# Weights subtracted a quarter earlier, candidate tiles laid out cell by cell, two one-column copies gone, in a one-core audio tower kernel

## The chip, the cores and the metric

One core of a Trainium2 chip runs the whole program. The metric is device time in microseconds. The engines are PE (TensorE), ACT (ScalarE), DVE (VectorE), POOL (GpSimd) and SP (SyncE, which issues the DMAs). Each works through its own list of instructions in order and meets the others at semaphores.

## The reference

The input is 32 clips of 40000 samples. The output has a row of 128 for each of 313 frames of each clip.

```python
h = _L0_tok_ref(x)                                  # frames of 128 samples, each times a DCT basis
h = h + _L0_attn_ref(_layernorm(h, axis=-1))        # softmax(x x^T) x inside each clip
h = h + _L0_ffn_ref(_layernorm(h, axis=-1), ...)    # below; H = 8 heads, K = 16, 64 keys a half
...
s0 = einsum(_l2norm(q0), _l2norm(keys0)); s1 = einsum(_l2norm(q1), _l2norm(keys1))
sc0, ix0 = top_k(s0, K); sc1, ix1 = top_k(s1, K)
cs = (sc0[..., :, None] + sc1[..., None, :]).reshape(b, s, H, K * K)
ci = (ix0[..., :, None] + ix1[..., None, :]).reshape(b, s, H, K * K)
fs, pos = top_k(cs, K)
fi = take_along_axis(ci, pos, axis=-1)
w = softmax(fs, axis=-1)
out = einsum('bshk,bshko->bso', gelu(<hidden, expert_down[fi]>) * w, expert_up[fi])
```

The index of an expert is the sum of two numbers below 64, so only experts 0 to 126 are used.

## The kernel before

The clips are worked in 16 pairs. A pair is 626 rows, cut into NT = 5 tiles of 128 rows (t = 0 to 4; the last overlaps). All engines follow one written order, `drive`: for each pair k, tile t and quarter p = 0 to 3 they do `slot(k, t, p)`, the feed-forward part, and then `front(k + 1, t, p)`, the DCT, attention and projection of the next pair. What an engine does in a quarter is given by `if p == ...` lines in its own `slot`, so the order of the lines sets the order of its work.

A tile goes through the slots with a lag. `exists(k, t, lag)` says that slot t works on the tile of `lag` slots ago:

- Lag -1: PE makes `SC`, the scores of all 16 half heads against their keys, and ACT copies them into `sraw`.
- Lag 0, DVE, p = 1 and 2: the best 16 of 64 for each half head (`vals`, `idx`), by MAX8, MATCH_REPLACE8 into `hrest`, MAX8, and two FIND_INDEX8.
- Lag 1: POOL builds 54 candidate sums a head, `cs` (p = 0) and `ci` (p = 1), with `cells`, five instructions each. DVE (p = 3) takes the best 16 of the 54: a MAX8 into `top`, MATCH_REPLACE8 into `crest`, MAX8, and MATCH_REPLACE8 into `c2`, eight of each, one a head. In `c2` each picked candidate has the value PICKED. The profile calls `c2` just `c`.
- Lag 2: ACT makes `zexp`, the mask `m` out of `c2`, and `wexp` = exp(cs) (p = 0). POOL (p = 2) makes `wz` = wexp times 1/sum, `Yw` = wz times m, and `Ye` = ci times m in bf16. PE (p = 3, in `rows`) turns Ye into the bank `EB` and Yw into the bank `U`, both with cells on partitions.
- Lag 3: ACT makes `hi` out of EB (p = 0), DVE makes `lo`, `alpha` and `beta` out of it (p = 1). The weights in U are split into three bf16 parts: ACT copies `wp` part 0 out of U, PE subtracts it in U by a matmul with `minusb` (`less(buf, 0)`), ACT copies part 1, PE subtracts it, ACT copies part 2. This is the subtraction chain, with semaphores w1_full, rest1_full, w2_full, rest2_full, w3_full. POOL (p = 3) multiplies the three parts with beta into `bw`, three instructions, waiting for w3_full.
- Lag 4: PE multiplies alpha and bw into `QB`, 16 matmuls a quarter ("quads"), and ACT copies each quarter into `WD`.
- Lag 5: POOL sums WD and multiplies it with the gelu values into `G`, ACT spreads G into `Gd`, PE multiplies with the expert rows and adds the residual (`FO`, in a QB bank), ACT copies to `ofin`, SP stores it.

In the front part `FB` is a pair of PSUM banks that PE and ACT hand to and fro: transposes, the attention's S (L421) and O (L429), in slot t = 3 at p = 0 the projection L440 with ACT's squares `sq` (L656), at (3, 2) the matmuls for variances and norms (L449 and L450, here called VAR), which DVE waits for at `v` (L985).

All candidate tiles except Yw and Ye have the layout [128, H, NC], 54 candidates of a head side by side. Yw and Ye are [128, NC, H], and the multiplications write them with a step.

Of the kernel before, what the change touches and what calls it, by code (L numbers as in the profile page):

```python
# [11 lines left out]
ALU = mybir.AluOpType  # L12
# [9 lines left out]
NT = 5  # L22
# [6 lines left out]
NC = 54  # L29
# [50 lines left out]
def build(nc, x, Wq, bq, ln_g, ln_b, keys0, keys1, down, up, ident_d, dct_d, indc_d, sel_d, row8_d, sel3_d, out):  # L80
# [4 lines left out]
    with ctx:  # L85
# [77 lines left out]


        sraw = sb("sraw", [128, 3, 1024])
        mark = sb("mark", [128, 2 * NT])
        hrest = sb("hrest", [128, 1024])
        vals = sb("vals", [128, 3, 16, TOP])
        idx = sb("idx", [128, 3, 16, TOP], U32)
        idxf = sb("idxf", [128, 16, TOP])  # L170
        vs = sb("vs", [128, 16, TOP])
        cs = sb("cs", [128, 3, H, NC])
        ci = sb("ci", [128, 3, H, NC])
        crest = sb("crest", [128, H, NC])
        c2 = sb("c2", [128, H, NC])
        top = sb("top", [128, H, TOP])
        zexp = sb("zexp", [128, H, TOP])
        zs = sb("zs", [128, H])
        rz = sb("rz", [128, H])
        m = sb("m", [128, H, NC])  # L180
        wexp = sb("wexp", [128, H, NC])
        wz = sb("wz", [128, H, NC])
        Yw = sb("Yw", [128, NC, H])
        Ye = sb("Ye", [128, NC, H], BF16)
        wp = sb("wp", [128, 3, 3, 256], BF16)
# [186 lines left out]
        def _(pe):  # L372
# [130 lines left out]
            def slot(k, t, p):  # L503
                n = NT * k + t
                if p == 0 and t == NT - 1 and exists(k, 0, 0):
                    inner(k)
                if p == 1 and exists(k, t, -1):
                    k1, t1 = (k, t + 1) if t < NT - 1 else (k + 1, 0)
                    scores(k1, t1)
                if p == 1 and exists(k, t, 3):  # L510
                    pe.wait_ge(s["w1_full"], n - 2)
                    less(RING[(t - 3) % NT], 0).then_inc(s["rest1_full"], 1)
                if p == 2 and exists(k, t, 3):
                    pe.wait_ge(s["w2_full"], n - 2)
                    less(RING[(t - 3) % NT], 1).then_inc(s["rest2_full"], 1)
                if p == 3 and exists(k, t, 5):

                    after(pe, s["wd_full"], 4 * (n - 4) + 2 if exists(k, t, 4) else 4 * NTILES)
                    pe.wait_ge(s["gd_full"], n - 4)
                    pe.wait_ge(res_full[RING[t]], 16 * ring_use(k - 1, t) + 16)  # L520
                    for y in range(NY):
                        mm(FO, Gd[:, y, :], upR[:, y, :], start=(y == 0), stop=False)  # L522
                    mm(FO, ident[:], res[:, RING[t], :], start=False, stop=True).then_inc(s["fo_full"], 1)
                if exists(k, t, 4):
                    buf = RING[(t - 4) % NT]
                    if p == 0:
                        pe.wait_ge(s["alpha_full"], n - 3)
                        pe.wait_ge(s["bw_full"], n - 3)
                    bank = QB[p % 2]
                    after(pe, s["wd_full"], 4 * (n - 4) + p - 1)  # L530
                    bwv = bw[:, buf, :, :].rearrange("p s (a g q) -> p s a g q", a=2, g=NG)
                    for u in range(8):
                        for a in range(2):
                            last = mm(bank[:, 48 * u:48 * u + 48], alpha[:, buf, a, :, 8 * p + u],  # L534
                                      bwv[:, :, a, :, 8 * p + u], start=(a == 0), stop=(a == 1))
                    last.then_inc(s["quads_full"], 1)
                if p == 3 and exists(k, t, 2):
                    after(pe, s["lo_full"], n - 2)
                    pe.wait_ge(s["y_full"], n - 1)
                    rows(Ye, identb, STE, True).then_inc(s["eb_full"], 1)  # L540
                    after(pe, s["w3_full"], n - 2)
                    rows(Yw, ident, U[:, 0:256], False).then_inc(s["st_full"], 1)
# [33 lines left out]
        def _(act):  # L576
# [91 lines left out]
            def slot(k, t, p):  # L668
# [7 lines left out]
                if p == 0 and exists(k, t, 2):  # L676
                    buf = RING[(t - 2) % NT]
                    act.wait_ge(s["c2_full"], n - 1)
                    after(act, s["zs_full"], n - 2)
                    A(zexp[:], top[:], ACT.Exp).then_inc(s["zexp_full"], 1)  # L680
                    after(act, s["y_full"], n - 2)
                    A(m[:], c2[:], ACT.Relu, scale=-1.0, bias=cpick[:]).then_inc(s["m_full"], 1)
                    after(act, s["wz_full"], n - 2)
                    A(wexp[:], cs[:, buf, :, :], ACT.Exp).then_inc(s["wexp_full"], 1)
                if p == 0 and exists(k, t, 3):
                    buf = RING[(t - 3) % NT]
                    act.wait_ge(s["st_full"], n - 2)
# [22 lines left out]
                if p == 1 and exists(k, t, -1):  # L710
# [1 line left out]
                    act.wait_ge(s["scores_full"], n + 2)  # L712
                    after(act, s["halves_full"], n)
                    A(sraw[:, buf, :], SC[:], ACT.Copy).then_inc(s["sraw_full"], 1)  # L714
                if p == 1 and exists(k, t, 3):
                    act.wait_ge(s["rest1_full"], n - 2)
                    A(wp[:, RING[(t - 3) % NT], 1, :], U[:, 0:256], ACT.Copy).then_inc(s["w2_full"], 1)  # L717
                if p == 2 and exists(k, t, 3):
                    act.wait_ge(s["rest2_full"], n - 2)
                    A(wp[:, RING[(t - 3) % NT], 2, :], U[:, 0:256], ACT.Copy).then_inc(s["w3_full"], 1)  # L720
                if exists(k, t, 4):
                    act.wait_ge(s["quads_full"], 4 * (n - 4) + p + 1)
                if p == 3 and exists(k, t, 5):
# [4 lines left out]
                if exists(k, t, 4):  # L728
                    if p == 0:
                        after(act, s["ws_steps"], 2 * (n - 5))  # L730
                    blocks = QB[p % 2][:, 0:384].rearrange("p (u s g) -> p s u g", u=8, g=NG)
                    for g in range(NG):
                        r = slice(32 * g, 32 * g + 32)
                        last = A(WD[r, RING[(t - 4) % NT], :, 8 * p:8 * p + 8], blocks[r, :, :, g], ACT.Copy)  # L734
                    last.then_inc(s["wd_full"], 1)

            def late(t, p):
                if (t, p) == (0, 0):
# [15 lines left out]
        def _(pool):  # L754
# [79 lines left out]
            def cells(dst, v, done):  # L834

                halves = v.rearrange("p (h a) r -> p h a r", a=2)
                for i0, ni, nj, off in CAND:
                    by = "p h (j i) -> p h i j" if i0 == 4 else "p h (i j) -> p h i j"
                    o = dst[:, :, off:off + ni * nj].rearrange(by, i=ni)
                    a0 = halves[:, :, 0, i0:i0 + ni].unsqueeze(3).to_broadcast([128, H, ni, nj])  # L840
                    a1 = halves[:, :, 1, 0:nj].unsqueeze(2).to_broadcast([128, H, ni, nj])
                    last = tt(o, a0, a1, ALU.add)  # L842
                last.then_inc(done, 1)


            def slot(k, t, p):
# [10 lines left out]
                if p == 0 and exists(k, t, 1):  # L857
                    buf = RING[(t - 1) % NT]
                    pool.wait_ge(s["halves_full"], n)
                    kk, t1 = (k, t - 1) if t else (k - 1, NT - 1)  # L860
                    pool.wait_ge(s["rn_steps"], 12 * kk + 12)
                    after(pool, s["cs_full"], n - 1)
                    tt(vs[:], vals[:, buf, :, :], rn[:, 16 * t1:16 * t1 + 16].unsqueeze(2).to_broadcast([128, 16, TOP]), ALU.mult
                       ).then_inc(s["vs_full"], 1)
                    pool.wait_ge(s["vs_full"], n)
                    after(pool, s["wexp_full"], n - 2)
                    cells(cs[:, buf, :, :], vs[:], s["cs_full"])
                if p == 0 and t == 0 and exists(k, t, 0):
                    pool.wait_ge(s["seed4_full"], k + 1)
                    newton(y4[:], xh4[:], na[:], c15[:], s["rn_steps"], 12 * k, rn[:])  # L870
# [6 lines left out]
                if p == 2 and exists(k, t, 2):  # L877
                    buf = RING[(t - 2) % NT]
                    pool.wait_ge(s["rz_full"], n - 1)
                    pool.wait_ge(s["wexp_full"], n - 1)  # L880
                    tt(wz[:], wexp[:], rz[:].unsqueeze(2).to_broadcast([128, H, NC]), ALU.mult).then_inc(s["wz_full"], 1)
                    pool.wait_ge(s["wz_full"], n - 1)
                    pool.wait_ge(s["m_full"], n - 1)
                    after(pool, s["st_full"], n - 2)
                    for Y, src in ((Yw, wz[:]), (Ye, ci[:, buf, :, :])):
                        last = tt(Y[:].rearrange("p c h -> p h c"), src, m[:], ALU.mult)  # L886
                    last.then_inc(s["y_full"], 1)
                if p == 3 and exists(k, t, 3):
                    buf = RING[(t - 3) % NT]
# [13 lines left out]
        def _(dve):  # L903
# [103 lines left out]
            def slot(k, t, p):  # L1007
                n = NT * k + t
                if p == 0 and exists(k, t, 0):


                    dve.wait_ge(s["sraw_full"], n + 1)
                    after(dve, s["cs_full"], n - 1)
                    after(dve, s["idxf_full"], n - 1)
                    V.tensor_copy(mark[:, t:t + 1], ident[:, 0:1])
                if exists(k, t, 0) and p in (1, 2):
                    buf = RING[t]
                    chain = s["top_chain"]
# [48 lines left out]
                if p == 3:  # L1067
                    if exists(k, t, 1):
                        buf = RING[(t - 1) % NT]
                        dve.wait_ge(s["cs_full"], n)  # L1070
                        after(dve, s["wexp_full"], n - 1)
                        V.tensor_copy(mark[:, NT + t:NT + t + 1], ident[:, 0:1])
                        chain = s["cand_chain"]
                        for h in range(H):
                            V.max(top[:, h, 0:8], cs[:, buf, h, 0:NC8]).then_inc(chain, 1)
# [5 lines left out]
                            V.max(top[:, h, 8:16], crest[:, h, :]).then_inc(chain, 1)  # L1081
                        for h in range(H):
                            dve.wait_ge(chain, 2 * H + h + 1)
                            V.match_replace(c2[:, h, :], top[:, h, 8:16], crest[:, h, :], PICKED
                                            ).then_inc(chain if h < H - 1 else s["c2_full"], 1)
                    if exists(k, t, 0):
                        dve.wait_ge(s["top_chain"], 79)
# [89 lines left out]
```

## Time and profile before

| what | value |
|---|---|
| median of 3 runs | 2089.96 us (2086.35 to 2092.89) |
| the profiled execution | 2086.75 us |
| its span, first to last instruction | 2084.9 us |
| mean granted clock of TensorE | 0.77 of full |
| DVE busy | 1924.9 us, 92% |
| PE busy | 1702.7 us, 82% |
| POOL busy | 1561.5 us, 75% |
| ACT busy | 1214.0 us, 58% |

Busy times are shares of the whole span. The span has a beginning of about 110 us and an end of about 75 us in which not every engine has work. Instructions of one engine overlap at their ends, so an instruction's own duration is longer than what it takes of its engine's queue; the distance to the start of the next tells that.

### The profile page before, as it was taken

How to read it: one execution, taken by the hardware profiler on the slowest of the kernel's cores; microseconds unless marked ns; L12 is line 12 of the kernel's file. 1: busy time of each engine (PE TensorE's matmuls, PEld its weight loads, DVE VectorE, ACT ScalarE, POOL GpSimd, SP SyncE). 2: the span in 40 equal slices, each digit the busy share in tenths (PEclk: the TensorE clock that was granted, in tenths of full speed). 3: DMA queues.
4: the chain of work that ended last, by engine and by line, in shares of the span. 5: the costliest groups of instructions: out<-in, count | busy, mean ns of one | idle time of the engine just before them, and what ended most of it. 6: DMA issues, size and time to landing. Idle time of an engine off the chain costs nothing.

```text
span 2084.9 us, 49107 instructions
## 1 busy us (share of the span) xinstructions
PE 1702.7 (82%) x11935; PEld 1301.7 (62%) x11935; DVE 1924.9 (92%) x15878; ACT 1214.0 (58%) x3835; POOL 1561.5 (75%) x2561
## 2 busy tenths in 40 slices
PE   5567888878888888888888888888888888798766
PEld 3335576756767676675667667576665767567556
DVE  3299999999999999999999999999999999999992
ACT  3345656666565656656566665666665566665454
POOL 2238787886868788686878868778777878878765
PEclk9676878778777877887788678778867887787666
DMA  1000000000000000000000000000000000000000
GB/s 35 13 9 2 19 7 8 19 7 19 7 19 7 7 19 9 19 7 18 7 6 19 9 17 8 13 13 6 19 7 18 9 13 13 6 13 9 7 6 11
DMA packets 46676, 24.93 MB, mean 12 GB/s; under 512 B 4955, under 2 KB 46116, under 8 KB 46390
## 3 DMA queue, kind: packets, MB, share of 16 engines
q1 hardware_dynamic: 46390, 21.80, 3.8%
q8 instruction: 96, 1.57, 0.3%
q14 instruction: 190, 1.56, 0.2%
HBM read 11.52 MB, written 10.26 MB: 10 GB/s over the span
## 4 chain that ended last, share of the span: by engine, by line
PE 43%; DVE 23%; ACT 18%; POOL 10%; issue 5%; SPq 0%; another core or an unknown queue 0%; DMA 0%; POOLq 0%; DVEq 0%; ACTq 0%
PE QB L534 9%; PE FB L449 5%; PE SC L483 5%; ACT WD L734 4%; PE FB L440 4%; PE QB L522 4%; DVE alpha L1048 4%; DVE idx L1032 3%; DVE idx L1035 3%; DVE hrest L1026 3%; PE FB L429 3%; ACT hi L674 3%; PE FB L421 2%; POOL sa L764 2%; PE FB L397 2%
## 5 line engine op out<-in xcount | busy, mean ns | idle before, releaser
L894 POOL TENSOR_TENSOR bw<-beta,wp 128x1024 bf16<-128x1024 bf16 x240 | 508.0, 2147 | 121.3 <-ACT wp L720 121.3
L534 PE MATMUL QB<-bw,alpha 128*128 128x48 bf16 x5120 | 554.1, 277 | 32.2 <-issue 32.2
L534 PEld LDWEIGHTS QB<-bw,alpha 128*128 128x128 bf16 x5120 | 522.1, 151 | 69.9 <-issue 60.9
L734 ACT ACTIVATE WD<-QB 32x96 f32<-32x96 f32 x1280 | 307.0, 240 | 77.6 <-PE QB L534 66.1
L1048 DVE TENSOR_SCALAR alpha<-hi 128x1024 bf16<-128x1024 bf16 x640 | 276.0, 503 | 0.0
L483 PE MATMUL SC<-WK,hidT 128*128 128x512 f32 x320 | 228.8, 805 | 50.2 <-ACT stdT L666 36.3
L1032 DVE FIND_INDEX8 idx<-vals,sraw 128x8 uint32<-128x64 f32 x1280 | 250.9, 219 | 0.0
L1035 DVE FIND_INDEX8 idx<-vals,hrest 128x8 uint32<-128x64 f32 x1280 | 250.5, 219 | 0.0
L1026 DVE MATCH_REPLACE8 hrest<-vals,sraw 128x64 f32<-128x64 f32 x1280 | 249.6, 207 | 0.0
L842 POOL TENSOR_TENSOR ci<-idxf 128x64 f32<-128x64 f32 (+3 forms) x400 | 124.0, 345 | 121.2 <-DVE beta L1054 121.1
L727 ACT ACTIVATE ofin<-QB 128x128 f32<-128x128 f32 x80 | 22.2, 277 | 282.3 <-PE QB L534 279.6
L842 POOL TENSOR_TENSOR cs<-vs 128x64 f32<-128x64 f32 (+3 forms) x400 | 172.5, 467 | 6.3
L886 POOL TENSOR_TENSOR Ye<-ci,m 128x432 bf16<-128x432 f32 x80 | 174.8, 2186 | 0.0
L1023 DVE MAX8 vals<-sraw 128x8 f32<-128x64 f32 x1280 | 169.1, 208 | 0.0
L1030 DVE MAX8 vals<-hrest 128x8 f32<-128x64 f32 x1280 | 167.2, 207 | 0.0
L483 PEld LDWEIGHTS SC<-WK,hidT 128*128 128x128 f32 x320 | 72.9, 247 | 110.9 <-issue 54.4
L714 ACT ACTIVATE sraw<-SC 128x1024 f32<-128x1024 f32 x80 | 83.0, 1037 | 99.8 <-PE SC L484 99.0
L440 PE MATMUL FB<-hidTn,WcT 128*128 128x313 f32 x256 | 112.1, 589 | 34.2 <-ACT sq L656 23.4
L522 PE MATMUL QB<-upR,Gd 128*128 128x128 f32 x640 | 134.6, 378 | 4.5 <-issue 4.2
L674 ACT ACTIVATE hi<-EB,cdig 128x256 bf16<-128x256 f32 x320 | 124.9, 475 | 22.8 <-PE EB L494 21.7
L501 PE MATMUL U<-wp,minusb 128*128 128x256 bf16 x160 | 51.0, 319 | 103.1 <-ACT wp L717 71.7
L522 PEld LDWEIGHTS QB<-upR,Gd 128*128 128x128 f32 x640 | 123.6, 284 | 9.1 <-issue 7.7
(206 smaller groups left out, 3999.2 us busy)
## 6 DMA issues: line engine op xcount, KB each, us to landing
res<-h_scratch SPq DMA_DIRECT2D x80, 64.0 KB, 1.8
xin<-in_x SPq DMA_DIRECT2D x32, 128.0 KB
h_scratch<-h2n SPq DMA_DIRECT2D x32, 128.0 KB
out<-ofin SPq DMA_DIRECT2D x64, 64.0 KB, 1.5
h_scratch<-h2n SPq DMA_DIRECT2D x32, 28.5 KB
out<-ofin SPq DMA_DIRECT2D x16, 57.0 KB
xin<-in_x SPq DMA_DIRECT2D x32, 28.0 KB
xin<-in_x SPq DMA_DIRECT2D x32, 0.2 KB
```

Of the source, the lines that this page charges most:

```text
L440: mm(bank[:, 0:NF], WcT[:, 128 * c:128 * c + 128], hidTn[:, NF * b:NF * b + NF], start=True, stop=True).then_inc(f_full[c % 2], 1)
L483: mm(SC[:, cols], hidT[:, START[t1]:START[t1] + 128], WK[:, cols], start=True, stop=False)
L522: mm(FO, Gd[:, y, :], upR[:, y, :], start=(y == 0), stop=False)
L534: last = mm(bank[:, 48 * u:48 * u + 48], alpha[:, buf, a, :, 8 * p + u], bwv[:, :, a, :, 8 * p + u], start=(a == 0), stop=(a == 1))
L674: last = A(hi[:, c, :], STE, ACT.Identity, bias=cdig[:, c:c + 1])
L734: last = A(WD[r, RING[(t - 4) % NT], :, 8 * p:8 * p + 8], blocks[r, :, :, g], ACT.Copy)
L842: last = tt(o, a0, a1, ALU.add)
L894: last = tt(bw[:, buf, NY * i:NY * i + NY, :], beta[:, buf, :, :], wp[:, buf, i, :].unsqueeze(1).to_broadcast([128, NY, 256]), ALU.mult)
L1026: V.match_replace(rest[i], vals[:, buf, i, 0:8], raw[i], -1e30).then_inc(chain, 1)
L1032: V.max_index(idx[:, buf, i, 0:8], vals[:, buf, i, 0:8], raw[i]).then_inc(chain, 1)
L1035: last = V.max_index(idx[:, buf, i, 8:16], vals[:, buf, i, 8:16], rest[i])
L1048: last = V.tensor_scalar(a8[:, :, :, xx, :], h8, BASE + float(NY * xx), None, ALU.is_equal)
```

## The change

Three things are changed. First, `c2`, `ci`, `m`, `wexp` and `wz` get the layout [128, NC, H], a cell's eight heads side by side, as Yw and Ye have it already. `m`, `wz`, Yw and Ye become plain products of 432 values in a row. The instructions that write `c2` (DVE), `wexp` (ACT) and `ci` (POOL) now step by 8 values, 32 bytes, between neighbours; `cs` stays as it was. Second, the subtraction chain is one quarter earlier: `less(buf, 0)` and the copy of part 1 go from the start of p = 1 to the end of p = 0, `less(buf, 1)` and the copy of part 2 from the start of p = 2 to the end of p = 1. Third, DVE's copies into `mark`, one column each, two a slot, are gone, and `mark` with them.

```diff
-        mark = sb("mark", [128, 2 * NT])
...
-        ci = sb("ci", [128, 3, H, NC])
+        ci = sb("ci", [128, 3, NC, H])
         crest = sb("crest", [128, H, NC])
-        c2 = sb("c2", [128, H, NC])
+        c2 = sb("c2", [128, NC, H])
...
-        m = sb("m", [128, H, NC])
-        wexp = sb("wexp", [128, H, NC])
-        wz = sb("wz", [128, H, NC])
+        m = sb("m", [128, NC, H])
+        wexp = sb("wexp", [128, NC, H])
+        wz = sb("wz", [128, NC, H])
...
# PE, slot
-                if p == 1 and exists(k, t, 3):
-                    pe.wait_ge(s["w1_full"], n - 2)
-                    less(RING[(t - 3) % NT], 0).then_inc(s["rest1_full"], 1)
-                if p == 2 and exists(k, t, 3):
-                    pe.wait_ge(s["w2_full"], n - 2)
-                    less(RING[(t - 3) % NT], 1).then_inc(s["rest2_full"], 1)
...
                     last.then_inc(s["quads_full"], 1)
+                if p == 0 and exists(k, t, 3):
+                    pe.wait_ge(s["w1_full"], n - 2)
+                    less(RING[(t - 3) % NT], 0).then_inc(s["rest1_full"], 1)
+                if p == 1 and exists(k, t, 3):
+                    pe.wait_ge(s["w2_full"], n - 2)
+                    less(RING[(t - 3) % NT], 1).then_inc(s["rest2_full"], 1)
...
# ACT, slot
-                    A(wexp[:], cs[:, buf, :, :], ACT.Exp).then_inc(s["wexp_full"], 1)
+                    A(wexp[:].rearrange("p c h -> p h c"), cs[:, buf, :, :], ACT.Exp).then_inc(s["wexp_full"], 1)
...
# ACT: the copies of wp parts 1 and 2 move as on PE, to behind the WD copies of p = 0 and p = 1
...
# POOL, cells
-                    by = "p h (j i) -> p h i j" if i0 == 4 else "p h (i j) -> p h i j"
-                    o = dst[:, :, off:off + ni * nj].rearrange(by, i=ni)
+                    by = "p (j i) h -> p h i j" if i0 == 4 else "p (i j) h -> p h i j"
+                    o = dst[:, off:off + ni * nj, :].rearrange(by, i=ni)
...
# POOL, slot
-                    tt(wz[:], wexp[:], rz[:].unsqueeze(2).to_broadcast([128, H, NC]), ALU.mult).then_inc(s["wz_full"], 1)
+                    tt(wz[:], wexp[:], rz[:].unsqueeze(1).to_broadcast([128, NC, H]), ALU.mult).then_inc(s["wz_full"], 1)
...
-                        last = tt(Y[:].rearrange("p c h -> p h c"), src, m[:], ALU.mult)
+                        last = tt(Y[:], src, m[:], ALU.mult)
...
# DVE, slot
-                    V.tensor_copy(mark[:, t:t + 1], ident[:, 0:1])
...
-                        V.tensor_copy(mark[:, NT + t:NT + t + 1], ident[:, 0:1])
...
-                            V.match_replace(c2[:, h, :], top[:, h, 8:16], crest[:, h, :], PICKED
+                            V.match_replace(c2[:, :, h], top[:, h, 8:16], crest[:, h, :], PICKED
```

On ACT, slot t = 3 from `wexp` on: before, then with the change. Line numbers are those of each kernel's own text; the names after a wait are its semaphores.

```order
L684 ACTIVATE wexp<-cs 128x432 [waits wz_full]
L689 ACTIVATE wp<-U 128x256 [waits bw_full,st_full]
L701 ACTIVATE idxf<-idx,cquart 128x256 [waits ci_full,halves_full]
L734 ACTIVATE WD<-QB 32x12x8 [waits ws_steps,quads_full]
L734 ACTIVATE WD<-QB 32x12x8 x3
L656 ACTIVATE sq<-FB,bqc 128x313 [waits f0_full]
...
L714 ACTIVATE sraw<-SC 128x1024 [waits halves_full,scores_full]
L717 ACTIVATE wp<-U 128x256 [waits rest1_full]
L734 ACTIVATE WD<-QB 32x12x8 [waits quads_full]
L734 ACTIVATE WD<-QB 32x12x8 x3
L720 ACTIVATE wp<-U 128x256 [waits rest2_full]
```

With the change:

```order
L683 ACTIVATE wexp<-cs 128x8x54 [waits wz_full]
L688 ACTIVATE wp<-U 128x256 [waits bw_full,st_full]
L700 ACTIVATE idxf<-idx,cquart 128x256 [waits ci_full,halves_full]
L727 ACTIVATE WD<-QB 32x12x8 [waits ws_steps,quads_full]
L727 ACTIVATE WD<-QB 32x12x8 x3
L731 ACTIVATE wp<-U 128x256 [waits rest1_full]
L655 ACTIVATE sq<-FB,bqc 128x313 [waits f0_full]
...
L713 ACTIVATE sraw<-SC 128x1024 [waits halves_full,scores_full]
L727 ACTIVATE WD<-QB 32x12x8 [waits quads_full]
L727 ACTIVATE WD<-QB 32x12x8 x3
L734 ACTIVATE wp<-U 128x256 [waits rest2_full]
```

The copy of part 1 has moved ahead of the front's `sq` and of `sraw`; the copy of part 2 stands right behind the WD copies of p = 1, ahead of whatever front work there is. `wexp` has a three-dimensional output.

On PE, a slot t = 0 from the first quads on, before:

```order
L534 MATMUL QB<-bw,alpha 128x48 [waits wd_full,bw_full,alpha_full]
L534 MATMUL QB<-bw,alpha 128x48 x15
L483 MATMUL SC<-WK,hidT 128x512 [waits sraw_full,gelu_full,stdT_full,hidT_full]
L484 MATMUL SC<-bKs,stdT 128x512
L483 MATMUL SC<-WK,hidT 128x512
L484 MATMUL SC<-bKs,stdT 128x512
L501 MATMUL U<-wp,minusb 128x256 [waits w1_full]
L534 MATMUL QB<-bw,alpha 128x48 [waits wd_full]
L534 MATMUL QB<-bw,alpha 128x48 x15
L501 MATMUL U<-wp,minusb 128x256 [waits w2_full]
```

The same place with the change:

```order
L527 MATMUL QB<-bw,alpha 128x48 [waits wd_full,bw_full,alpha_full]
L527 MATMUL QB<-bw,alpha 128x48 x15
L500 MATMUL U<-wp,minusb 128x256 [waits w1_full]
L482 MATMUL SC<-WK,hidT 128x512 [waits sraw_full,gelu_full,stdT_full,hidT_full]
L483 MATMUL SC<-bKs,stdT 128x512
L482 MATMUL SC<-WK,hidT 128x512
L483 MATMUL SC<-bKs,stdT 128x512
L527 MATMUL QB<-bw,alpha 128x48 [waits wd_full]
L527 MATMUL QB<-bw,alpha 128x48 x15
L500 MATMUL U<-wp,minusb 128x256 [waits w2_full]
```

The first subtraction, with its wait for w1_full, now stands ahead of the scores. The second is at the end of its quarter instead of the start of the next; in slot t = 1 the 18 attention matmuls L429 lie between these two places.

## Rows read from the trace of the kernel before

**Rows 1.** The page: busy shares by engine; the chain's shares by engine.
```profile
PE 1702.7 (82%) x11935; PEld 1301.7 (62%) x11935; DVE 1924.9 (92%) x15878; ACT 1214.0 (58%) x3835; POOL 1561.5 (75%) x2561
...
PE 43%; DVE 23%; ACT 18%; POOL 10%; issue 5%; SPq 0%; another core or an unknown queue 0%; DMA 0%; POOLq 0%; DVEq 0%; ACTq 0%
```

**Rows 2.** Busy us of PE, PEld, DVE, ACT, POOL in one window; clock, DMA.
```profile
110.00:2010.00 1900.00, 1587.34 (x11283) 1216.76 (x11282) 1851.53 (x15427) 1139.49 (x3594) 1481.29 (x2396) 0.78 0.04 11
```

**Rows 3.** Waits: who waited for whom, us in total, times, longest.
```profile
PE EB L490 <- POOL Ye L886: 42.9, 19, 4.6
...
DVE v L985 <- PE FB L450: 38.3, 15, 21.6
...
DVE lo L1042 <- ACT hi L674: 35.8, 27, 9.1
```

**Rows 4.** The chain in order of time, one slot t=3: start, us, what.
```profile
1007.28 0.45 ACT wexp L684
1007.73 0.28 ACT wp L689
...
1009.29 0.53 ACT sq L656
```

**Rows 5.** The chain: first and last piece of wexp, Ye, c, U.
```profile
269.95 0.45 ACT wexp L684
...
2024.21 0.45 ACT wexp L684
...
332.26 2.11 POOL Ye L886
...
1807.15 2.08 POOL Ye L886
...
122.91 0.47 DVE c L1084 x3
...
2021.83 1.50 DVE c L1084 x9
...
276.01 0.12 PE U L501
...
2058.82 0.40 PE U L501
```

**Rows 6.** Timeline of DVE at a slot's end, and two groups of MAX8.
```profile
1001.41 0.19 DVE L1084 MATCH_REPLACE8 c<-top,crest 128x54 f32<-128x54 f32 x1
1001.53 0.14 DVE L1015 COPY mark<-ident 128x1 f32<-128x1 f32 x1
1001.59 0.21 DVE L1023 MAX8 vals<-sraw 128x8 f32<-128x64 f32 x1
...
L1081 DVE MAX8 top<-crest 128x8 f32<-128x54 f32 x640 | 81.5, 201 | 0.0
...
L1075 DVE MAX8 top<-cs 128x8 f32<-128x38 f32 x640 | 70.8, 184 | 0.0
```

**Rows 7.** Groups of POOL's products: busy us, mean ns, idle before, releaser.
```profile
L894 POOL TENSOR_TENSOR bw<-beta,wp 128x1024 bf16<-128x1024 bf16 x240 | 508.0, 2147 | 121.3 <-ACT wp L720 121.3
...
L886 POOL TENSOR_TENSOR Ye<-ci,m 128x432 bf16<-128x432 f32 x80 | 174.8, 2186 | 0.0
...
L886 POOL TENSOR_TENSOR Yw<-wz,m 128x432 f32<-128x432 f32 x80 | 90.2, 1127 | 6.3
...
L881 POOL TENSOR_TENSOR wz<-wexp,rz 128x432 f32<-128x432 f32 x80 | 72.7, 909 | 2.3 <-DVE rz L1066 2.3
...
L851 POOL TENSOR_TENSOR ws<-WD 128x128 f32<-128x128 f32 x80 | 39.6, 495 | 23.3 <-ACT WD L734 23.3
```

**Rows 8.** Timelines: DVE's alpha twice, and bw in a slot t=1.
```profile
1007.05 3.51 DVE L1048 TENSOR_SCALAR alpha<-hi 128x1024 bf16<-128x1024 bf16 x8
...
1106.22 2.76 DVE L1048 TENSOR_SCALAR alpha<-hi 128x1024 bf16<-128x1024 bf16 x8
...
1096.40 6.32 POOL L894 TENSOR_TENSOR bw<-beta,wp 128x1024 bf16<-128x1024 bf16 x3 [5.20 <-ACT wp L720]
```

More of the change, by code:

```diff
@@ L714, in slot @@
                     A(sraw[:, buf, :], SC[:], ACT.Copy).then_inc(s["sraw_full"], 1)
[L715 to L720, printed above, removed]
                 if exists(k, t, 4):
@@ L735, in slot @@
                     last.then_inc(s["wd_full"], 1)
+                if p == 0 and exists(k, t, 3):
+                    act.wait_ge(s["rest1_full"], n - 2)
+                    A(wp[:, RING[(t - 3) % NT], 1, :], U[:, 0:256], ACT.Copy).then_inc(s["w2_full"], 1)
+                if p == 1 and exists(k, t, 3):
+                    act.wait_ge(s["rest2_full"], n - 2)
+                    A(wp[:, RING[(t - 3) % NT], 2, :], U[:, 0:256], ACT.Copy).then_inc(s["w3_full"], 1)
             def late(t, p):
@@ L866, in slot @@
                     after(pool, s["wexp_full"], n - 2)
-                    cells(cs[:, buf, :, :], vs[:], s["cs_full"])
+                    cells(cs[:, buf, :, :].rearrange("p h c -> p c h"), vs[:], s["cs_full"])
                 if p == 0 and t == 0 and exists(k, t, 0):
```

## The prediction

> **What bounds the kernel now.** I read the page's engine shares first, then one long window, then the waits, then the chain of work that ended last. VectorE (DVE) is busy 1924.9 of 2084.9 us, PE 1702.7, and the chain still runs mostly through PE, 43%, with DVE 23%, ACT 18% and POOL 10% of it [rows 1]. The window from 110 to 2010 us shows why one should not stop at the 92%: there DVE is busy 1851.5 of 1900 us, 97.4%, and idles 48.5 us in all [rows 2]. The other idle time lies in the first 110 and the last 75 us. So two lines of work are nearly tied. One is DVE's own queue. The other goes PE, ACT, PE, ACT inside each slot and meets DVE where DVE waits: for `hi` before `lo` (35.8 us, 27 times) and for the VAR matmuls before `v` (38.3 us, 15 times) [rows 3]. In the chain's own order the second line shows its links: after `hi` come `m`, `wexp` (0.45), the first `wp` copy (0.28), then WD, and only then `sq` at 1009.29, whose FB bank the next projection matmul takes [rows 4]. A longer `wexp`, or one more ACT instruction ahead of `sq`, moves all of that.
>
> How often each touched instruction is a link, counted over the chain of the whole span: `wexp` in 39 pieces, one a slot, from 269.95 to 2024.21; Ye in 12, from 332.26 to 1807.15; the c2 replacements in 28 pieces of 23.8 us together, which at 1.47 us for one slot's eight is 16 slots or 130 replacements; the subtraction matmuls on U in 69 pieces of 9.8 us [rows 5]. A change of a link's length, times its count, is the first estimate of the change of the span. The DVE queue is a second account, which may grow only until its 48.5 us of idle are used, if the waits let it.
>
> **The two copies.** One stands between a replacement that starts at 1001.41 and the MAX8 behind it: the copy starts at 1001.53, MAX8 at 1001.59, so it takes 0.06 us of DVE's queue, though its row says 0.14 [rows 6]. I take as much for both kinds: 160 x 0.06 = 9.6 us off DVE's account, and, with DVE 23% of the chain, 2 us off the chain. The waits they carried go to the first MAX8, so no wait changes.
>
> **Steps of 32 bytes.** c2 is now written one head at a time into [NC, H]: 54 values, each 32 bytes behind the last. So is `wexp`, 432 values, by ACT, and `ci` by POOL. No row of DVE or ACT shows such a write. Contiguous, a DVE replacement of 54 takes 0.12 us from its start to the next load [rows 6]. The nearest rows are POOL's. Yw is written in just these steps and takes 1127 ns for 432 values, 2.6 ns each; `wz`, contiguous with one full-length input, takes 909; `ws` with two full inputs takes 495 for 128, so Yw may be slow from reading alone [rows 7]. Ye is the row that speaks for a price: two-byte values at 16-byte steps take 2186 ns, 5.1 ns each, where contiguous `bw` takes 2147 for 1024, 2.1 ns each [rows 7]. A writer that hops can therefore be the limit here. The bounds: below, nothing; above, one write every 2.6 ns, all of Yw. A gain has no reason, since nothing else of these instructions changes. ACT: `wexp` (432 values) and `wp` (256) differ by 0.17 us, 0.97 ns a value [rows 4], so the bound is (2.6 - 0.97) x 432 = +0.70 us. DVE: MAX8 over 54 and over 38 values differ by 17 ns, 1.06 ns a value [rows 6], so the bound is 1.54 x 54 = +83 ns a replacement. I take 0.64 for ACT, whose instruction is long (a little under the bound, since some of Yw's 1127 ns is its start), and 60 ns for DVE, where some writes can finish under the next value load, because Ye's row is nearer to a price than to none. Chain: 39 x 0.64 = +25.0; 130 x 0.060 = +7.8. DVE's account: 640 x 0.060 = +38.4.
>
> The Trainium skill, Vector Engine (DVE) Microarchitecture Reference, section Measured stream behaviour, speaks against this edit outright: a DVE port keeps its full rate only in runs of two or more adjacent words, and a destination that steps 24 words every element took 2.50 ns a column where contiguous took 1.05. By that page the replacements would cost 1.45 x 54 = 78 ns each, an estimate, +50 us on DVE's account instead of 38. No run here shows it yet.
>
> **Y, wz and ci on POOL.** Ye loses its steps and becomes a product of the shape of Yw: 2186 - 1127 = 1.06 us shorter, with a lower end of 2186 - 909 = 1.28 [rows 7]. Yw keeps two full inputs; 0 to -0.2, taken as 0. `wz` stays. `ci` gets steps: 0 to +0.2 us a tile (the 909 to 1127 gap), taken 0.1. PE waited 42.9 us for Ye in 19 slots [rows 3], and it is a link in 12: 12 x (1.06 - 0.1) = -11.5 us. The other 68 tiles' gain is POOL idle, for POOL is busy 78% of the window [rows 2].
>
> **The subtraction chain.** Each of its four instructions goes one step of the order earlier. Where the change pays is POOL: `bw` waited 121.3 us for the third `wp` copy [rows 7], nearly all in slots t=1, where the O matmuls stood between: `bw` starts at 1096.40 after 5.20 us idle [rows 8]. Now it can start right behind Ye. But that wait is not on the chain, where `bw` hardly occurs; what it brings is that POOL's cs work is over before `alpha` starts in t=2. There eight `alpha` take 3.51 us beside cs, and 2.76 us where they are alone [rows 8]: 0.75 x 16 = -12 us at best on DVE's account, 9 taken. On PE the first subtraction leaves the place between the scores and the second group of quads: half of its 9.8 us of links, -5. It now waits ahead of the front's matmuls for the first `wp`, until 1008.0 in [rows 4], so PE stands there longer; what hides it is that `sq` at 1009.29 has yet to free the FB bank. If that cover went, PE would lose about the length of `wexp` and `wp`, 0.7 us a slot, or 1.3 with the price above. On ACT the second `wp` copy now stands ahead of `sq`, E or hidT: +0.28 [rows 4] in the slots where these are links, three of four of the 39, +8.1. In t=2 ACT is the link all through and order changes nothing.
>
> **The sum.** Chain: +25.0 + 7.8 - 2 - 11.5 - 5 + 8.1 = +22.4 us. DVE's account: +38.4 - 9.6 - 9 = +20, which fits under 48.5. The profiled execution took 2086.75 us with a span of 2084.9, so about 2109 by that execution; the median of the three runs is 3.2 us above it. Forecast 2112 us, 1.1% slower.
>
> **The rivals.**
> - *Steps are free* (faster). Place: the port writes of c2, `wexp`, `ci`. For it: POOL's `ws` explains Yw without them. Then 22.4 - 25.0 - 7.8 - 1.2 = -11.6: 2078 us, and 2070 if DVE's 18 us come through in full. It decides from the price per value: the rest of the sum is -11.6, the stepped links are 39 x 432 + 130 x 54 = 23,900 values, so below 0.48 ns extra per value the kernel gets no slower. Chance 0.25.
> - *Half the price* on both engines: 0.32 x 39 + 0.03 x 130 + 0.6 - 11.6 = +5: 2095 us. Chance 0.15.
> - *Only DVE pays.* The long ACT instruction hides its writes. Chain -2.6, DVE's account +20, partly under its idle: 2087 to 2095, 2090. Chance 0.08.
> - *The lines add.* DVE's 20 us and the chain's 22 do not overlap, because the chain changes lines several times in five slots; or the subtraction, waiting for `wp`, holds up the scores in t=0. +42: 2132 us. For it: the tie is close, 48.5 us in 80 tiles. Chance 0.10.
> - The forecast: 0.42, own range 2102 to 2124.
>
> **The numbers.** Within 0.3%, some 6 us, a measurement of this kernel can't tell a change. Slower: 0.42 of the forecast, 0.12 of half, 0.10 of the adding lines, 0.01 of DVE only: 0.65. Same: 0.03 + 0.06 + 0.02 from the edge of the free case: 0.11. Faster: 0.24. The range reaches into the free case and to the adding lines: 2074 to 2136.
>
> **What would show it.** `wexp` near 1.2 us (0.57 before means free); the c2 replacement near 0.18 us from start to next load; Ye near 1.1 us; `bw` no longer waiting for `wp` in t=1, `alpha` in t=2 near 2.8 us; DVE busy higher by 25 to 30 us; the waits of `lo` and `v` about as long as before. The forecast is wrong if `wexp` keeps its length, or if POOL's earlier start lets `alpha` collide somewhere else.

## The result and the profile after

The changed kernel takes 2113.5 us (median of 4 runs, 2112.6 to 2119.4) where the kernel before, run beside it, takes 2088.5 (2086.4 to 2092.9): a ratio of 1.0123, 95% interval 1.0097 to 1.0149, 25 us slower. Forecast were 2112 us. The profiled execution took 2119.4 us. Its page:

```profile
span 2117.6 us, 48947 instructions
...
PE 1775.7 (84%) x11935; PEld 1349.2 (64%) x11935; DVE 1905.5 (90%) x15718; ACT 1247.8 (59%) x3835; POOL 1505.8 (71%) x2561
...
PE 53%; ACT 22%; DVE 15%; POOL 5%; issue 4%; SPq 0%; DMA 0%; another core or an unknown queue 0%; ACTq 0%; POOLq 0%; DVEq 0%
```

Beside [rows 1]: the last line is the chain by engine. PE is busy 73 us longer with the same 11,935 matmuls, DVE is busy 19 us shorter, and the chain runs through PE and ACT more (53% and 22%, from 43% and 18%) and through DVE less. The long window says the same, with its columns as in [rows 2]:

```profile
110.00:2040.00 1930.00, 1656.55 (x11270) 1260.63 (x11268) 1830.59 (x15273) 1170.94 (x3585) 1429.13 (x2403) 0.75 0.04 11
```

DVE now idles 99 of 1930 us, where it idled 48.5 of 1900, and the granted clock is 0.75 instead of 0.78. The waits answer to [rows 3] and to the wait of `bw` in [rows 7]:

```profile
PE U L500 <- ACT wp L688: 143.0, 63, 4.6
...
PE FB L439 <- ACT sq L655: 2.1, 3, 0.7
...
POOL bw L893 <- ACT wp L734: 93.8, 43, 4.2
...
DVE v L984 <- PE FB L449: 66.8, 15, 22.5
...
DVE lo L1040 <- ACT hi L673: 58.3, 45, 8.3
```

DVE waits longer at both of its meeting places with the PE and ACT line: 67 us for VAR and 58 for `hi`, from 38 and 36. PE's 143 us for the first `wp` copy belong to the subtraction that now stands ahead of the front's matmuls. They are not all new. In the kernel before, PE waited 103 us at its two subtractions, and 23 for `sq`:

```profile
PE U L501 <- ACT wp L717: 71.7, 34, 3.5
PE U L501 <- ACT wp L689: 31.4, 16, 2.0
PE FB L440 <- ACT sq L656: 23.4, 15, 2.2
```

The wait for `sq` is down to 2 us, so part of the new wait only stands in its place. Last the touched instructions, by form (busy us, mean ns, idle before them, releaser):

```profile
L482 PE MATMUL SC<-WK,hidT 128*128 128x512 f32 x320 | 240.5, 844 | 39.2 <-ACT stdT L665 32.4 <-ACT hidT L660 4.8 <-ACT sraw L713 1.2
...
L1081 DVE MATCH_REPLACE8 c<-top,crest 128x54 f32<-128x54 f32 x640 | 122.6, 246 | 0.0
...
L885 POOL TENSOR_TENSOR Ye<-ci,m 128x432 bf16<-128x432 f32 x80 | 89.7, 1121 | 0.0
...
L885 POOL TENSOR_TENSOR Yw<-wz,m 128x432 f32<-128x432 f32 x80 | 89.5, 1119 | 6.3
L880 POOL TENSOR_TENSOR wz<-wexp,rz 128x432 f32<-128x432 f32 x80 | 89.0, 1113 | 2.4 <-DVE rz L1064 2.4
...
L683 ACT ACTIVATE wexp<-cs 128x432 f32<-128x432 f32 x80 | 80.0, 1001 | 0.0
```

Ye fell from 2186 to 1121 ns, `wexp` rose from 569 to 1001, `wz` from 909 to 1113, and the scores matmul from 805 to 844.

How much of an instruction's length its queue feels is read from starts. After, ACT's timeline at p = 0 of a slot t=3 and DVE's in the c2 replacements (start, us, what):

```profile
1022.65 0.99 ACT L683 ACTIVATE wexp<-cs 128x432 f32<-128x432 f32 x1
1023.42 0.44 ACT L688 ACTIVATE wp<-U 128x256 bf16<-128x256 f32 x1
1023.74 0.51 ACT L700 ACTIVATE idxf<-idx,cquart 128x256 f32<-128x256 uint32 x1
...
1015.08 0.24 DVE L1081 MATCH_REPLACE8 c<-top,crest 128x54 f32<-128x54 f32 x1
1015.19 0.08 DVE L1081 MATCH_VALUE_LOAD c<-top,crest 128x8 f32 x1
1015.26 0.24 DVE L1081 MATCH_REPLACE8 c<-top,crest 128x54 f32<-128x54 f32 x1
```

From the start of `wexp` to that of `wp` it is now 0.77 us (in the same place of the kernel before 0.46, from 1007.16 to 1007.62), and from `wp` to `idxf` 0.32 (0.26): in all about 0.38 us more of ACT's queue in a slot. From a replacement to the next load it is 0.11 us, as the 0.12 of [rows 6], and from one replacement to the next 0.18, as before. A replacement of the kernel before, one ahead of that in [rows 6]:

```profile
1001.23 0.19 DVE L1084 MATCH_REPLACE8 c<-top,crest 128x54 f32<-128x54 f32 x1
```

The mean duration of a replacement grew by 46 ns, from 200 to 246. That is not the step: in the first experiment below, which has no step at all, it is 255. No run here tells what sets it.

### The profile page after: what moved, and what is told of

The parts are those of the page before. It is cut to its first block, busy times and chain, and to the rows that moved or that the text cites. A ratio compares the mean times of both kernels' runs of the same rounds, so it can differ in the third digit from the quotient of the medians.

```text
span 2117.6 us, 48947 instructions
## 1 busy us (share of the span) xinstructions
PE 1775.7 (84%) x11935; PEld 1349.2 (64%) x11935; DVE 1905.5 (90%) x15718; ACT 1247.8 (59%) x3835; POOL 1505.8 (71%) x2561
## 4 chain that ended last, share of the span: by engine, by line
PE 53%; ACT 22%; DVE 15%; POOL 5%; issue 4%; SPq 0%; DMA 0%; another core or an unknown queue 0%; ACTq 0%; POOLq 0%; DVEq 0%
PE QB L527 13%; PE SC L482 6%; PE FB L439 6%; PE FB L448 5%; PE QB L515 5%; ACT WD L727 4%; PE FB L428 4%; PE FB L420 3%; ACT hi L673 3%; ACT wexp L683 3%; DVE idx L1030 2%; DVE idx L1033 2%; DVE hrest L1024 2%; PE FB L396 2%; PE U L493 2%
## 5 line engine op out<-in xcount | busy, mean ns | idle before, releaser
L482 PE MATMUL SC<-WK,hidT 128*128 128x512 f32 x320 | 240.5, 844 | 39.2 <-ACT stdT L665 32.4
L1046 DVE TENSOR_SCALAR alpha<-hi 128x1024 bf16<-128x1024 bf16 x640 | 264.0, 484 | 0.0
L439 PE MATMUL FB<-hidTn,WcT 128*128 128x313 f32 x256 | 131.0, 681 | 7.4 <-ACT hidTn L650 5.3
L448 PE MATMUL FB<-indc,sq 128*128 128x24 f32 x640 | 130.3, 352 | 0.7 <-ACT sq L655 0.7
L448 PEld LDWEIGHTS FB<-indc,sq 128*128 128x128 f32 x640 | 125.8, 291 | 1.2 <-ACT sq L655 1.1
```

The source lines that it names most:

```text
L439: mm(bank[:, 0:NF], WcT[:, 128 * c:128 * c + 128], hidTn[:, NF * b:NF * b + NF], start=True, stop=True).then_inc(f_full[c % 2], 1)
L448: mm(bank[:, 40 * tt:40 * tt + 24], sq[:, c, cols], indc[:, c, :], start=(c == 0), stop=(c == 3))
L482: mm(SC[:, cols], hidT[:, START[t1]:START[t1] + 128], WK[:, cols], start=True, stop=False)
L1046: last = V.tensor_scalar(a8[:, :, :, xx, :], h8, BASE + float(NY * xx), None, ALU.is_equal)
```

## The experiments

Each ratio is to the kernel before, run beside it on the same chip, with its 95% interval. The time of a kernel is its median. Where a gain or a loss is given once, the ratio and the medians agree on it within 2 us. No kernel here leaves out or changes a value that is computed; the two with a pad do one copy more.

**Marks.** The kernel before without the two `tensor_copy` into `mark`.

> Only the two one-column copies are dropped. By the count of links (DVE is 23% of the chain) the span falls by about 2 us, 2086 to 2088; the DVE queue gets 9 to 10 us shorter in its rows. A rival: DVE is the bound at 97.4%, then the whole 9 us come through, 2079.

1.0002 [0.9994, 1.0011], 12 runs: neither the 2 us nor the 9 that were expected. DVE, 97% busy in the long window, gave up 160 instructions, 9.6 us of its queue by the estimate, for nothing. The replacements of this kernel, which are written without a step:

```profile
L1081 DVE MATCH_REPLACE8 c<-top,crest 128x54 f32<-128x54 f32 x640 | 123.2, 255 | 0.0
```

**The chain of subtractions alone**, both steps as in the diff.

> Only the subtraction chain is moved, layouts and copies as before. Theory A, that the time went into PE standing at its first subtraction (143 us of waits in the changed kernel's profile, 63 times) with the scores or the front's matmuls behind it: this kernel takes most of the loss, 2103 to 2112. Theory B, that the loss is the longer wexp on ACT, with the moved chain worth only the +8 - 5 us of the forecast: 2088 to 2095.

1.0065 [1.005, 1.008]: slower by 13.5 us, between the two expected ranges.

**The layout alone.**

> Only the layouts are changed. wexp is 0.32 us longer in the queue (39 links: +12), wp part 0 0.06 (+2), Ye 1.07 shorter and wz 0.20 longer (12 links: -10). Theory A: about +4 us, 2086 to 2096. Theory B: most of the loss, 2103 to 2112. The replacement into c2 costs DVE nothing, as in the changed kernel: start to next load 0.116 us.

1.0189 [1.0165, 1.0212]: a loss beyond both expectations, and more than that of the whole change. The five runs lie apart, two at 2120 and 2125 us and three from 2134 to 2137, so that the loss is 39 us by the ratio and 45 by the medians (2133.9 against 2088.6). The chain, which costs time alone, gives some 14 to 20 us back on top of this.

**The second step alone**: `less(buf, 1)` and the copy of part 2 at the end of p = 1, the first step as before.

> Only the second subtraction and the copy of part 2 are moved, to the end of p = 1; the first stays at the start of p = 1. PE then does not wait for wp part 0 ahead of the scores, and bw in t = 1 starts about 5 us earlier. Theory A: no loss, 2080 to 2090, and alpha in t = 2 near 2.8 us for eight. If moving anything of the chain costs (ACT order), 2095 or more.

0.9946 [0.993, 0.9961]: faster by 11 us, a little more than expected. The waits of POOL and DVE in this kernel:

```profile
POOL bw L894 <- ACT wp L735: 39.2, 24, 4.2
DVE lo L1042 <- ACT hi L674: 34.7, 30, 9.1
DVE v L985 <- PE FB L450: 34.5, 15, 22.6
...
PE U L501 <- ACT wp L717: 97.5, 34, 4.4
```

`bw` waits 39 us instead of 121, and neither of DVE's two waits is longer. PE waits 98 us for the copy of part 1 instead of 72, and that costs nothing that shows in the time. This is the half in which no instruction newly comes ahead of `sq`, E or `hidT`. How the 11 us come about is not shown: the eight `alpha` of t = 2 got shorter (3.61 to 3.03 us on average), but others got longer, and all `alpha` together take 273.2 us, from 276.0.

**The changed kernel with `wexp` as it was**, [128, H, NC], and the step on POOL:

```
-  A(wexp[:].rearrange("p c h -> p h c"), cs[:, buf, :, :], ACT.Exp)
+  A(wexp[:], cs[:, buf, :, :], ACT.Exp)
-  tt(wz[:], wexp[:], rz[:]...to_broadcast([128, NC, H]), ALU.mult)
+  tt(wz[:].rearrange("p c h -> p h c"), wexp[:], rz[:]...to_broadcast([128, H, NC]), ALU.mult)
```

> The changed kernel with wexp alone back in its old layout, written contiguous. Theory C: the moved first subtraction's +0.6% remains and no more: 2090 to 2100. Theory D: 2110 to 2120 as the changed kernel.

0.9952 [0.9933, 0.9971], 2077.5 us, with runs from 2061 to 2085 and below both expectations: one write pattern on ACT, with 0.09 us less of `wz` on POOL, is 36 us.

**The layout with `wexp` as it was**, the same edit and no chain moved.

> The layout change alone (the run with it all took 1.9% more), but wexp keeps its layout and ACT writes it contiguous; POOL writes wz with the step instead, and c2, ci, m as in the changed kernel. Theory C: the longer wexp (queue +0.32 us, the copy behind it +0.06) delays ACT's sq, E and hidT, PE stands longer, and is granted the low clock more often: without it the loss goes and the shorter Ye remains, 2076 to 2090, mean clock 0.76 or more, scores matmul L483 near 800 ns. Theory D: the loss comes from POOL or DVE's side of the layout (an earlier Ye or ci that shifts the phases): 2115 or more, clock near 0.73.

0.9924 [0.9909, 0.994], 2071.3 us, faster than expected. Its page, and two groups by form:

```profile
PE 1674.8 (81%) x11935; PEld 1296.4 (63%) x11935; DVE 1910.5 (92%) x15878; ACT 1215.3 (59%) x3835; POOL 1479.7 (72%) x2561
```

```profile
L881 POOL TENSOR_TENSOR wz<-wexp,rz 128x432 f32<-128x432 f32 x80 | 80.9, 1012 | 2.7 <-DVE rz L1066 2.7
...
L684 ACT ACTIVATE wexp<-cs 128x432 f32<-128x432 f32 x80 | 45.3, 566 | 0.0
```

All other steps are still in this kernel: c2's on DVE, `ci`'s and `wz`'s on POOL. The rest of the layout is a gain of 16 us, and the difference to the layout alone, 55 us by the ratios and 62.6 by the medians, is `wexp`'s (with 0.1 us more of `wz`).

**Only `wexp` in the new layout**, everything else as before, `wz` reading it with a step.

> The kernel before, with only wexp in the cell-by-cell layout (ACT writes it with steps of 32 bytes, POOL reads it with them into wz as before). Theory C: it is slower by most of the layout's loss, 2110 to 2135, clock 0.73 to 0.75. Theory D: by the 39 links x 0.38 us at most, 2090 to 2103, clock as before, 0.77.

1.0295 [1.0275, 1.0314], 2150.3 us: +62 us, from the other side, and more than the largest loss expected. `wz`, which here reads with the step, is 0.23 us longer, and only 0.1 us longer between the two layout kernels, whose difference is nearly the same; so `wz` does not carry it. Its page:

```profile
PE 1796.3 (84%) x11935; PEld 1354.3 (63%) x11935; DVE 1924.4 (89%) x15878; ACT 1245.7 (58%) x3835; POOL 1575.4 (73%) x2561
...
L483 PE MATMUL SC<-WK,hidT 128*128 128x512 f32 x320 | 265.6, 927 | 36.2 <-ACT stdT L666 22.3
```

ACT is busy 32 us longer, but PE 94 us longer, with the same matmuls. One place where this comes in, first as the chain in order of time, then as a window of 5 us (columns as in [rows 2]) and as PE's timeline:

```profile
1037.22 0.88 ACT wexp L684
1038.11 0.21 ACT wp L689
...
1039.61 0.53 ACT sq L656
...
1040.18 1.34 PE FB L440 x4
1041.52 1.71 PE SC L483 x2
1043.22 0.43 PE SC L484
1043.65 1.48 PE SC L483 x2
```

```profile
1040.00:1045.00 5.00, 4.82 (x10) 2.19 (x11) 4.97 (x42) 2.69 (x8) 3.83 (x8) 0.66 0.00 0
...
1040.18 1.34 PE L440 MATMUL FB<-hidTn,WcT 128*128 128x313 f32 x4 [1.89 <-ACT sq L656]
```

`sq` starts 2.39 us after `wexp`, against 2.01 in [rows 4]: the 0.38. Behind it the projection takes 1.34 us, and then the scores run at half the clock: 1.71 and 1.48 us for a pair of matmuls. The same place of the kernel before, in the same views:

```profile
1010.00:1015.00 5.00, 5.00 (x29) 3.41 (x30) 4.96 (x40) 3.68 (x9) 3.74 (x8) 1.00 0.00 0
...
1009.86 1.32 PE L440 MATMUL FB<-hidTn,WcT 128*128 128x313 f32 x4 [1.51 <-ACT sq L656]
```

```profile
1011.18 0.86 PE SC L483 x2
1012.04 0.22 PE SC L484
1012.26 0.86 PE SC L483 x2
```

Here the granted clock is 1.00 and a pair takes 0.86. PE stood 1.51 us for `sq` ahead of the projection before, and 1.89 with the long `wexp`: the 0.38 again, now on PE. Behind the longer wait TensorE ran at 1.2 instead of 2.4 GHz. The Trainium skill, TensorE: Matmul & The Clock Gate, section What's actually happening, ties the level to how busy the engine has been just before. That agrees in direction with these two rows, but no row here shows which wait decides. Nor is it shown that the lower clock is part of the price: the last experiment has a lower clock and no price.

**The same time without steps**: a copy of 256 contiguous values, once right behind `wexp` at p = 0 and once at p = 2 behind the WD copies.

```
+  A(pad[:], WcT[:, 0:256], ACT.Copy)
```

> The kernel before with one more ACT instruction a slot right behind wexp: a contiguous copy of 256 columns into a tile that nobody reads, about 0.3 to 0.4 us of ACT's queue, no steps anywhere. Theory C1, that any delay of ACT at that place costs a multiple of itself: 2120 to 2150, clock 0.73 to 0.75. Theory D1, that the stepped writes do harm beyond their own time: 2090 to 2105, clock 0.77.

> The same extra ACT instruction, but behind the WD copies of p = 2, where ACT mostly idles before ofin. If place is what counts: 2086 to 2094, clock 0.77. If ACT's total work counts: as the kernel with the instruction behind wexp.

The copy's group in the first of the two:

```profile
L686 ACT ACTIVATE pad<-WcT 128x256 f32<-128x256 f32 x80 | 33.4, 418 | 0.0
```

At p = 0 1.0105 [1.0087, 1.0122], +21 us for some 0.31 us of queue in each of 80 slots (25 us); at p = 2 1.0029 [1.0006, 1.0051], +5 (its eight runs lie between 2086 and 2104). ACT is busy 59 and 60% of the span, so the place decides and not the amount. That the price at p = 0 goes through what is queued behind it there, `sq`, E and `hidT`, is the reading of the rows above and not tested one by one. The time with the copy at p = 0, 2108.1 us, lies between its two expected ranges; that at p = 2 is as expected for a price of the place.

**PE's half of the first step**: `less(buf, 0)` at the end of p = 0, no ACT instruction moved.

> The kernel before with only PE's first subtraction moved to the end of p = 0; ACT copies part 1 where it did. If the cost of the moved chain is PE standing at that wait ahead of the scores: 2098 to 2108, as when the chain moved alone. If it is ACT's copy ahead of sq and E: 2084 to 2092.

PE's waits at the two subtractions and for `sq` in this kernel:

```profile
PE U L501 <- ACT wp L689: 102.0, 49, 4.2
...
PE U L501 <- ACT wp L717: 52.6, 19, 3.2
...
PE FB L440 <- ACT sq L656: 3.3, 8, 0.4
```

1.0014 [1.0005, 1.0024], +3 us. PE waits 155 us at its subtractions instead of 103, and 3 for `sq` instead of 23: the earlier wait is partly covered by one that was there, and what is left costs next to nothing.

**The best parts together**: the layout with `wexp` flat, the second step alone, no marks.

> What the runs point to: only the second subtraction moved, the copies into mark dropped, cell-by-cell layout for c2, ci, m and wz, wexp left as it was. Theory C: the gain of the second subtraction (-0.5%) and of the shorter Ye: 2062 to 2076. Theory D: 2100 or more.

0.9889 [0.9872, 0.9907], 2063.9 us. The busy times from its page:

```profile
PE 1672.2 (81%) x11935; PEld 1295.2 (63%) x11935; DVE 1907.6 (93%) x15718; ACT 1213.6 (59%) x3835; POOL 1481.7 (72%) x2561
```

**And `wexp` moved out of p = 0** in that kernel, to the start of p = 1.

> The best kernel so far (second subtraction moved, no mark copies, cell-by-cell layout but wexp as it was), with wexp also taken out of p = 0: ACT makes it at the start of p = 1, behind the front's sq, E or hidT. If 0.45 us of ACT at p = 0 is worth a multiple of itself in the other direction too: 2035 to 2055. If DVE is the bound by then (busy 93% of the span there): 2056 to 2066.

0.9907 [0.9874, 0.994], 2064.3 us: nothing more. Making a slot's p = 0 shorter than it was in the kernel before brought nothing, at least with `wexp` in this place; making it longer costs. The expected range for a bound by DVE holds the time, but the chain of this kernel is 51% PE and 19% DVE. Its page:

```profile
PE 1729.4 (84%) x11935; PEld 1325.0 (64%) x11935; DVE 1904.4 (92%) x15718; ACT 1215.7 (59%) x3835; POOL 1464.0 (71%) x2561
```

PE is busy 57 us longer than in the kernel before this one, with the same matmuls, and the mean granted clock is 0.747 instead of 0.785. The time is the same. A lower clock and a longer busy time of PE are then not by themselves a price.

## Why the forecast came out, and where it was wrong

The sign and the total were right, and the cause that carried the total, the stepped write of `wexp` on ACT's path to `sq`, is shown by three kernels (the changed one, the layout, and the one before, each with and without it: 36, 55 to 63, and 62 us). The forecast named this write and its place as the largest term, and the direction follows from that. That the total came within 2 us is luck: the steps of the sum were off in both directions and partly cancelled.

- **Length of `wexp`.** Taken 0.64 us, measured 0.32 on its queue and 0.06 on the instruction behind it. The bound from Yw's row, one write every 2.6 ns, was the wrong neighbour: Yw takes 1119 ns without a step, so its length is that of two full inputs, as the rival of the free steps said. ACT pays 0.73 ns extra a value (0.32 us over 432), above the 0.48 at which that rival put the break-even.
- **Worth of it.** "A change of a link's length, times its count" gave 39 x 0.38 = 15 us; measured 36 to 62. The chain after has `wexp` in 60 pieces, the one of the `wexp` kernel in 46, and where the layout has it flat in 22: the count moves with the length. Even all 80 slots give 30 us. The pad fits the 80: 25 us by the queue, 21 measured. The lower clock goes along with the rest of `wexp`'s price, as the rows above show for one slot, but is not shown to be its cause. Why 0.38 us with steps cost 62 and 0.31 without cost 21 is not settled; a pad of 0.38 was not tried, and `wz` is 0.23 us longer in the `wexp` kernel.
- **c2 on DVE.** Taken 60 ns each, +38.4 us; measured 0 on the queue: replacements start 0.18 us apart before and after. DVE's busy time fell by 19 us instead of rising by 25 to 30; `alpha` gave 12 of it (276.0 to 264.0 us), and the copies the rest (7.5 us less in the kernel without them). The Trainium skill, Vector Engine (DVE) Microarchitecture Reference, section Measured stream behaviour on trn2, has a figure for steps of 24 words, and the estimate from it was 78 ns. For these writes of 54 values at steps of 8 words the trace does not agree: 11 to 12 hundredths of a us from start to next load before and after. Ye's row, taken as the nearer one, was a POOL row of two-byte values, and said nothing of DVE.
- **The marks.** -2 us on the chain was in truth 0 within 0.1%, and with it falls the second account: DVE's queue was not the bound, although it was 97.4% busy.
- **Ye, `wz` and `ci`.** Ye 1.07 us shorter, as forecast, and its links went from 12 to 3. `wz` was not in the sum: it grew by 0.20 us when it got the layout without steps, and by 0.10 with a stepped write and a flat `wexp`. Its second input, `rz`, repeats eight values over the cells instead of each value 54 times. The flat-`wexp` layout, -16 us, is the measured value of the whole item beside the forecast's -11.5.
- **The chain of subtractions.** Forecast: -5 for PE, +8.1 for the copy ahead of `sq`, and nothing from POOL but `alpha`. Measured +13.5 for both. By subtraction, and so argued and not shown, the copy is worth 13.5 - 3 + 11 = +21 us, close to the pad's +21 of almost the same length in the same quarter: again 80 slots and not 29. But parts do not add here: the whole first step, PE's half and the copy, is 25 us by this subtraction and 13 between the last two kernels that differ by it (2077.5 and 2063.9). The second step brought 11 us, which the sum had not. `bw` did not stop waiting: it waits 94 us in the changed kernel, from 121, namely 26 in t=1 (96 before), 25 in t=3 (nothing before) and 38 in t=4 (21 before). In the t=1 of [rows 8] the idle time ahead of it fell from 5.20 to 2.24 us. The eight `alpha` of t=2 span 2.88 us on average over 16 slots, 3.61 before, as forecast, and all `alpha` together 12.0 us less, also as forecast; but in the layout kernel with the flat `wexp`, where the chain is not moved, they are down to 2.94 in t=2 as well, so the earlier chain need not be what does it. The two rows of [rows 8] do not carry this reading: the 3.51 us stand in a slot t=3, and there it is 3.61 in the changed kernel, and the 2.76 stand in a slot t=2. The timelines after:

```profile
1111.92 6.31 POOL L893 TENSOR_TENSOR bw<-beta,wp 128x1024 bf16<-128x1024 bf16 x3 [2.24 <-ACT wp L734]
...
1022.40 3.61 DVE L1046 TENSOR_SCALAR alpha<-hi 128x1024 bf16<-128x1024 bf16 x8
...
1125.44 2.75 DVE L1046 TENSOR_SCALAR alpha<-hi 128x1024 bf16<-128x1024 bf16 x8
```

- **The waits of `lo` and `v`.** Forecast as before; they grew by 22 and 28 us, together as much as the 51 us that DVE idles more in the long window. They are the place where the loss arrives at DVE.
- **The rival of the held-up scores.** Its wait came, its price did not: PE waits 143 us for the first `wp` copy in the changed kernel and 102 in the kernel that has the first subtraction alone, and that one costs 3 us.

**Parts don't add.** +62 for `wexp`, -16 for the rest of the layout, +13.5 for the chain and 0 for the marks make +59; the whole change is +25. With the long `wexp` the chain gives 20 us back by the medians (2133.9 to 2113.5) and 14 by the ratios, with the flat one it costs about 6 (2071.3 to 2077.5, where the runs lie far apart). A reason would be that with a long `wexp` an earlier `bw` and the copies' new places relieve the later quarters; no run tests it, and it stays open.

## What to carry to other kernels

Before pricing an edit by the links of the chain, ask what is queued behind it on its engine and who hands over to whom there: 0.3 us on an engine that is 58% busy cost 21 us ahead of the handoff to PE and 5 us two quarters later, while 160 instructions off an engine that was 97% busy brought nothing. Do not take the chain's own count of links (39) as the number of slots that pay, for it changes with the length; counting every slot in which the place exists came near for the pad (25 us against 21) and was still too low for `wexp` (30 against 62). When a layout has to step somewhere, put the step where the rows show it free or cheap, here DVE's `c2` (nothing) and POOL's `wz` (0.1 us), and keep the one on the path contiguous: that alone turned the layout from +1.9% to -0.8%, and with the second subtraction moved the kernel reached 2063.9 us, 1.1% under the kernel before.

## What the runs showed of the hardware

- A write of 432 fp32 values at 32-byte steps costs ACT 0.32 us of queue (0.73 ns a value) and the next ACT instruction 0.06; on POOL Yw takes 1127 ns with the same step and 1119 without; on DVE replacements of 54 such values start 0.18 us apart with the step and without. The length of a replacement moves by some 50 ns from kernel to kernel with no step anywhere (200 ns in the kernel before, 255 without the marks), so an instruction's own length alone is no sign of a price.
- On POOL the two-byte output at 16-byte steps (Ye) takes 2186 ns, without steps 1121. A product with two full fp32 inputs takes 2.6 ns a value whether its output steps or not.
- The same 11,935 matmuls kept PE busy 1672 us in the fastest kernel here and 1796 in the slowest, at mean granted clocks of 0.785 and 0.726; from the kernel before to the slowest, a delay of 0.38 us a slot on another engine moved PE's busy time by 94 us. Yet with `wexp` late PE was busy 1729 us at 0.747, and the time was that of the fastest within 1 us.
